# Layer 1's h split into three bf16 parts by word halves on two engines, and layer 2's edge loads issued later in a block

## The reference

```python
def _sage_conv(x, src, dst, W_l, b_l, W_r):
    agg = segment_sum(x[src], dst)
    cnt = segment_sum(ones, dst)
    return (agg / max(cnt, 1)[:, None]) @ W_l + b_l + x @ W_r

def L0(x):                       # node network
    h = relu(_sage_conv(x, src, dst, W_l1, b_l1, W_r1))      # layer 1
    h = relu(_sage_conv(h, src, dst, W_l2, b_l2, W_r2))      # layer 2
    return h @ W_out + b_out

def L1(x, edge_attr):            # edge network
    out = concat([x[src], edge_attr], axis=1)
    out = selu(out @ W1a + b1a) @ W1b + b1b
    mean = segment_sum(out, dst) / max(counts, 1)[:, None]
    h = concat([x, mean, u[0]], axis=1)
    return selu(h @ W2a + b2a) @ W2b + b2b

x = layernorm(x + L0(x))
x = layernorm(x + L1(x, edge_attr))
```

## Time and profile before

| | |
|---|---|
| median of 3 runs | 2545.67 us (2545.40 to 2546.12) |
| profiled execution | 2547.18 us |
| its span | 2545.4 us |
| mean granted TensorE clock | 0.917 of full speed |
| TensorE busy (matmuls) | 2084.5 us, 82% |
| VectorE busy | 1637.0 us, 64% |
| ScalarE busy | 1015.8 us, 40% |
| GpSimd busy | 1845.8 us, 73% |
| DMA | 342.56 MB, mean 135 GB/s |
| block of counts, load | 12 issues of 5488 KB seen, 18.7 us from issue to landing |

### The profile page before, as it was taken

How to read it: one execution, slowest core, us unless ns; L and a number is a source line. 1 busy time by engine, 2 the same in 40 slices (tenths; PEclk the granted TensorE clock), 3 DMA queues, 4 the chain that set the end, 5 groups by cost and what they waited for, 6 DMA issues and landing times. The chain is left out here.

```text
span 2545.4 us, 54296 instructions
## 1 busy us (share of the span) xinstructions
PE 2084.5 (82%) x19234; PEld 1539.5 (60%) x19234; DVE 1637.0 (64%) x3320; ACT 1015.8 (40%) x2319; POOL 1845.8 (73%) x1864
## 2 busy tenths in 40 slices
PE   1899999989989998984788888888878888867753
PEld 1555565555545555553676676777767777766753
DVE  6899999996455564554566666666666666643433
ACT  3787877874000000013344344444433444433322
POOL 5546768676777777777777777777777777777775
PEclk9999999999999999985899999998999999986665
DMA  8368786777769877824433333333333333332212
GB/s 298 111 231 224 228 264 180 250 198 134 210 208 253 237 210 232 241 59 109 123 74 74 71 80 74 77 76 72 76 77 74 80 74 74 72 71 51 51 41 46
DMA packets 524456, 342.56 MB, mean 135 GB/s; under 512 B 398996, under 2 KB 476495, under 8 KB 520781
## 3 DMA queue, kind: packets, MB, share of 16 engines
q1 hardware_dynamic: 407075, 267.01, 38.2%
q0 software_dynamic: 54240, 57.31, 10.3%
q10 hardware_dynamic: 62890, 14.87, 2.9%
HBM read 201.55 MB, written 137.36 MB: 133 GB/s over the span
## 5 line engine op out<-in xcount | busy, mean ns | idle before, releaser
L987 POOL DMA_INDIRECT A_sb<-source_terms,src_cur x1092 | 1049.1, 961 | 332.9 <-issue 327.4
L938 POOL DMA_INDIRECT sorted_edges<-pm_row,pm_to x520 | 575.4, 1107 | 183.6 <-issue 154.1
L1871 DVE TENSOR_TENSOR arena<-iota_code,arena 128x2048 f16<-128x2048 f16 (+1 forms) x392 | 435.5, 1179 | 19.6 <-PE cnt_ps L1416 17.3
L1082 ACT ACTIVATE A_sb<-cnt_ps 128x392 f32 (+1 forms) x784 | 383.8, 499 | 135.9 <-PE cnt_ps L1416 86.2
L1545 PE MATMUL agg_ps<-A_sb,arena 128*128 128x448 f16 x1911 | 378.6, 355 | 0.0
L1416 PEld LDWEIGHTS cnt_ps<-arena 128*128 128x128 f16 x3136 | 191.1, 100 | 225.7 <-issue 161.4
L1416 PE MATMUL cnt_ps<-arena 128*128 128x98 f16 x3136 | 280.3, 214 | 44.5 <-ACT A_sb L1082 27.1
L1545 PEld LDWEIGHTS agg_ps<-A_sb,arena 128*128 128x128 bf16 x1911 | 186.1, 99 | 165.0 <-issue 5.3
L1647 PE MATMUL agg_ps<-A_sb 128*65 128x48 f32 x2184 | 179.5, 243 | 123.1 <-DVE A_sb L2208 123.1
L1647 PEld LDWEIGHTS agg_ps<-A_sb 128*65 128x65 f32 x2184 | 165.7, 158 | 138.4 <-DVE A_sb L2208 130.4
L1423 PE MATMUL agg_ps<-A_sb,arena 128*65 128x448 f16 x686 | 243.3, 355 | 0.0
(11 more groups left out here) (308 smaller groups left out, 3505.7 us busy)
## 6 DMA issues: line engine op xcount, KB each, us to landing
counts_matrix<-A_sb SPq DMA_DIRECT2D x12, 5488.0 KB, 17.4
A_sb<-counts_matrix SPq DMA_DIRECT2D x12, 5488.0 KB, 18.7
arena<-in_edge_attr_dram SPq DMA_DIRECT2D x90, 256.0 KB
sorted_edges<-zrow SPq DMA_DIRECT2D x13, 1716.0 KB
arena<-sorted_edges SPq DMA_DIRECT2D x169, 128.0 KB
A_sb<-source_terms,src_cur POOLq DMA_INDIRECT x1092
overlapping_rows<-A_sb SPq DMA_DIRECT2D x1, 13056.0 KB, 39.4
pm_row<-in_edge_attr_dram ACTq DMA_DIRECT2D x46, 256.0 KB
```

The costliest lines, as they stand in the source:

```text
L938: pool.indirect_dma_start(out=sorted_d, out_offset=bass.IndirectOffsetOnAxis(ap=pm_to[:, k, j:j + 1], axis=0), in_=pm_row[:, k, j, :], in_ ...
L987: pool.indirect_dma_start(out=gath[k][:, j * F:(j + 1) * F], out_offset=None, in_=p_d, in_offset=bass.IndirectOffsetOnAxis(ap=src_cur[k][: ...
L1082: act.activation(Asb(half)[:, :, bass.ds((b * BG + k) * GROUP, GROUP)].rearrange("p b (w j) -> p b w j", j=PAIR), cnt_ps[k % 2][:, 0:SUB * ...
L1871: ins = dve.tensor_tensor(hot_rows[:, slots], iota_code[:, 0:n, :].unsqueeze(1).to_broadcast([P, AT_ONCE * SUB // 2, n, 2]), turned[:, bas ...
```

## The change

**The split.** The rounding is replaced by a cut: the first part is the upper 16 bits of each word of h, which is a bf16 number; the rest h minus this number is exact in f32, and its upper 16 bits are the second part; the rest of that gives the third. `h_rest` names the three f32 arrays (h in `hs`, the first rest in `iota_i`'s space, the second in `h1m[1]`, in the arena), and `h_top` their upper halves, read as bf16 with a stride of two. The two subtractions go to VectorE, as a new `split_h` at hot row 48 (SPLIT_AT) of superblocks 2 to 13; for block 12 behind the sort of group 17, and for block 13 behind the sum of the counts. GpSimd's `split_h` keeps three copies of upper halves into `hpart`; the second and third wait for VectorE's `rest_made`. `h_split` now counts three a block, and `store_h` waits for the third. VectorE's first subtract waits until the copies of the block before are done.

**The loads of layer 2.** ScalarE issues none ahead of the copy of `h2T` and none behind `move_agg2`. It issues one behind the copy of `h2T`, one behind the square root, and one ahead of `move_agg2`, or two there where the next superblock has four groups.

The diff, without the renaming of a semaphore and two changed totals (line numbers in the rows of the changed kernel are those after it):

```diff
--- before.py
+++ after.py
@@ -91,6 +91,7 @@
 FROM_SP = IN_STAGE1 + 3
 PLACE_AT = (16, 36)
 SLOT_AT = (32, 44)
+SPLIT_AT = 48
 END_PARTS = NSB - 3
 ENDS_IN = 16 * 2 * (END_PARTS + 2)
@@ -394,6 +395,9 @@
         st = sb("st", [CH, 4, NCH], F32)
         hr = iota_i[0:CH, :].bitcast(F32).rearrange("p (c f) -> p c f", f=H)
         zero_c = sb("zero_c", [CH, NCH], F32)
+        h_rest = [t.rearrange("p c f -> p (c f)") for t in (hs[:, :, :], hr, h1m[1])]
+        h_top = [t.bitcast(BF16).rearrange("p (n t) -> p n t", t=2)[:, :, 1] for t in h_rest]
+        h_out = [hpart[:, i].rearrange("p c f -> p (c f)") for i in range(3)]
         src_cur = [sb(f"src_cur{i}", [P, EJ], I32) for i in range(DEEP)]
         def halves(t):
@@ -586,7 +590,7 @@
                 sp.dma_start(Wedge[half * F:(half + 1) * F, half * F:(half + 1) * F], W1a[F:2 * F, :]).then_inc(w2_in, 16)
             def store_h(m, half):
-                sp.wait_ge(h_split, m + 1)
+                sp.wait_ge(h_split, 3 * m + 3)
                 sp.dma_start(by_node(h1_d, m), hs[:, :, :]).then_inc(h_stored, 16)
                 for part in range(3):
                     sp.dma_start(by_node(hp_d[part], m), hpart[:, part, :, :]).then_inc(h_stored, 16)
@@ -885,19 +889,11 @@
                 if not isinstance(m, int) or m > 0:
                     pool.wait_ge(h_stored, m * 64)
                 pool.sem_inc(pool_at, 1)
-                pool.tensor_copy(hpart[:, 0], hs[:, :, :]).then_inc(pool_dep, 1)
-                pool.wait_ge(pool_dep, m * 4 + 1)
-                pool.sem_inc(pool_at, 1)
-                pool.tensor_tensor(hr[:, :, :], hs[:, :, :], hpart[:, 0], ALU.subtract).then_inc(pool_dep, 1)
-                pool.wait_ge(pool_dep, m * 4 + 2)
-                pool.sem_inc(pool_at, 1)
-                pool.tensor_copy(hpart[:, 1], hr[:, :, :]).then_inc(pool_dep, 1)
-                pool.wait_ge(pool_dep, m * 4 + 3)
-                pool.sem_inc(pool_at, 1)
-                pool.tensor_tensor(hr[:, :, :], hr[:, :, :], hpart[:, 1], ALU.subtract).then_inc(pool_dep, 1)
-                pool.wait_ge(pool_dep, m * 4 + 4)
-                pool.sem_inc(pool_at, 1)
-                pool.tensor_copy(hpart[:, 2], hr[:, :, :]).then_inc(h_split, 1)
+                pool.tensor_copy(h_out[0], h_top[0]).then_inc(h_split, 1)
+                pool.wait_ge(rest_made, m * 2 + 1)
+                pool.tensor_copy(h_out[1], h_top[1]).then_inc(h_split, 1)
+                pool.wait_ge(rest_made, m * 2 + 2)
+                pool.tensor_copy(h_out[2], h_top[2]).then_inc(h_split, 1)
             gather_fine(0, FEW)
             pool.wait_ge(table_out, 16)
@@ -1158,14 +1154,14 @@
                 if not isinstance(m, int) or m < NSB - 1:
                     act.wait_ge(hT_turned, m + 1)
                     act.activation(hTs[:, :], t_ps[:, 0:SBN], ACT.Copy).then_inc(hT_moved, 1)
-                if s is not None and (s == 1 or LAYER2[s - 1] == 4):
-                    load_group(FIRST[s] + 2)
                 act.wait_ge(h2_turned, m + 1)
                 act.activation(h2T, t2_ps[:, 0:SBN], ACT.Copy).then_inc(h2_moved, 1)
                 if s is not None:
-                    load_group(FIRST[s] + 3)
+                    load_group(FIRST[s] + LAYER2[s] - 1)
                 act.wait_ge(var_ready, m + 1)
                 act.activation(st[:, 3, :], st[:, 2, :], ACT.Sqrt, bias=eps_t[0:CH, 0:1], scale=1.0 / F).then_inc(std_ready, 1)
+                if s is not None:
+                    load_group(FIRST[s + 1])
                 act.wait_ge(x2_turned, m + 1)
                 act.activation(x2T, cnt_ps[1][0:F, 0:SBN], ACT.Copy).then_inc(x2_moved, 1)
                 act.activation(x2all[:, bass.ds(at, 1), :, :].rearrange("p a c f -> p (a c) f"), x2c[:, :, :], ACT.Copy).then_inc(x2_kept, 1)
@@ -1173,9 +1169,10 @@
                     act.wait_ge(hT_turned, NSB)
                     act.activation(hTs[:, :], t2_ps[:, 0:SBN], ACT.Copy).then_inc(hT_moved, 1)
                 if s is not None:
-                    load_group(FIRST[s] + 4)
+                    load_group(FIRST[s + 1] + 1)
+                    if s + 1 < NSB and LAYER2[s + 1] == 4:
+                        load_group(FIRST[s + 1] + 2)
                     move_agg2(s)
-                    load_group(FIRST[s] + 5)
             def move_agg2(s):
                 act.wait_ge(agg2_ready, s + 1)
@@ -1905,6 +1902,10 @@
                     make_hot(s, half, begun, SLOT_AT[0])
                     begun = SLOT_AT[0]
                     own_terms(s - 2)
+                if s >= 2:
+                    make_hot(s, half, begun, SPLIT_AT)
+                    begun = SPLIT_AT
+                    split_h(s - 2)
                 make_hot(s, half, begun, SB_GROUPS)
             def grid(ap, f):
@@ -1928,6 +1929,14 @@
                 if m > 0:
                     dve.wait_ge(h_relu, m)
                 dve.tensor_tensor(hv[:, :, :], ht[:, :, :], grid(v_ps, H), ALU.add).then_inc(h_ready, 1)
+
+            def split_h(m):
+                dve.wait_ge(h_relu, m + 1)
+                if m > 0:
+                    dve.wait_ge(h_split, 3 * m)
+                dve.tensor_tensor(h_rest[1], h_rest[0], h_top[0], ALU.subtract).then_inc(rest_made, 1)
+                dve.wait_ge(rest_made, m * 2 + 1)
+                dve.tensor_tensor(h_rest[2], h_rest[1], h_top[1], ALU.subtract).then_inc(rest_made, 1)
             def layer(m, at=None):
@@ -2013,6 +2022,8 @@
             for q in range(IN_STAGE1, IN_STAGE1 + 3):
                 slot_group(q)
                 sort_group(q + 1)
+                if q == IN_STAGE1:
+                    split_h(NSB - 2)
             layer(NSB - 1)
@@ -2026,6 +2037,7 @@
             dve.wait_ge(layer_dve, 4 * NSB)
             inverses(0)
             dve.tensor_reduce(chk[0:CH, 0:1], all_counts, AX_X, ALU.add).then_inc(chk_made, 1)
+            split_h(NSB - 1)
             slot_group(IN_STAGE1 + 3)
             sort_group(IN_STAGE1 + 4)
             dve.wait_ge(chk_sum, 1)
```

6 lines of the change are left out of this document (3 added, 3 removed).

## The result

| | before | changed |
|---|---|---|
| median | 2545.9 us (4 runs) | 2599.9 us (4 runs, 2596.4 to 2601.6) |
| ratio | | 1.0206, 95% interval 1.0192 to 1.0221 |
| profiled execution, span | 2545.4 us | 2599.8 us |
| first scatter of group 18 | 652.02 us | 698.23 us |
| first gather | 1145.83 us | 1195.68 us |

The account below looks back on a forecast made before the run. VectorE was taken to bound the counting stage and GpSimd's scatters and gathers the rest from 652.0 us. Group 18 -1.1, loads -4.2 and hand-over -1.0 gave -6.3 us: 2545.7 to 2539.4 us, range 2531 to 2556.

Parts of the forecast that it names:

- The step that failed: Superblock 13's split: copies beside VectorE's work cost 0.4 us each, so split 11 is done at 598.8 us, 6.5 us later in the superblock.
- The step that turned it into time: Other superblocks of the counting stage: the later store and scatters cost nothing, the next `relu_h` coming some 25 us on.
- Rival C: Counting stage: each of GpSimd's three copies costs VectorE as much as a subtract, 0.9 us; 2556.2 us, slower; chance 0.16.
- The price of the copies on VectorE: Counting stage: GpSimd's three copies of a split cost VectorE 1.3 us a block, as the three casts did.
- The counting stage once the copies get in: Superblocks 2 to 12: 1.3 + 1.4 - 3.1 = -0.4 us a block, -4.4 us over 11 blocks.
- The end of split 11: In superblock 13: 6.5 us later in the superblock, 2.1 us later by the clock.
- the first scatter behind the blank: Group 16, behind the DMA that blanks `sorted_edges`: starts at 628.5 us instead of 626.41, 2.1 us later.
- Group 18: Start of its scatters, after groups 16 and 17 and a shorter split 13: 650.9 us instead of 652.02, -1.1 us.
- the sum of this part: The split's whole effect up to the start of group 18: -1.1 us.
- The hand-over's term: Before the gathers: part of GpSimd's 1.51 us wait for the stored source terms goes, -1.0 us (0 to 1.5).
- The loads' term: Layer 2: loads behind the copy of `h2T`, the block of counts having landed, end GpSimd's seven waits for slots, -4.2 us.
- 4 to 8 us at the next superblock's start, four times: Layer 2: TensorE waits this long where two loads precede `move_agg2` in superblocks 1, 4, 7 and 10, costing GpSimd nothing.

Follow-up runs that it names:

- one_input: Changed kernel plus one tiny single-input VectorE instruction behind the split's two subtracts; 2556.3 us against 2543.8 before, ratio 1.0043; on slower chips 0.9961.
- one_input_split_c: Changed kernel with a tiny single-input VectorE instruction behind the subtracts and layer 2's loads in their old places; 2549.6 us against 2541.2 before, ratio 1.0035.
- early_split_b: Changed kernel with the tiny single-input instruction, layer 2's loads in their old places and the subtracts at hot row 40; 2544.5 us against 2541.2 before, ratio 1.0017.

## Why the prediction was wrong, point by point

**The step that failed** is "six hot instructions from 584.98 us with one copy beside them ... two subtracts and the copy between them, 1.4 + 0.4, to 598.0; the last copy to 598.8 us". It prices a copy that must wait by the hot instruction in progress, as the old casts had to. In the changed kernel the copies of block 11 wait behind the second subtract, not in a run of hot instructions alone; the second copy ran from 636.89 to 642.07 us there, for 5.3 us in one other block and for 11.2 or 13.3 us in seven. In the old trace GpSimd's casts waited beside hot instructions only, and I took their 1.1 us for the rule. The page rule that the prediction put beside it (the Trainium skill, "SBUF — State Buffer", section "Who interferes with whom": the lock is held for a whole instruction) would have the copy wait 0.7 us for the subtract. The traces show 5 to 17 us; the measurement decides.

**The step that turned it into time** failed too: "In the other superblocks the later store and the later scatters cost nothing: the next `relu_h` comes some 25 us on". The prediction named what stands behind the split in SP's queue, the loads among them, and then asked only who needs `hs` next. The one who was near was VectorE, which sorts the loaded edges early in the next superblock, 13 us behind the subtracts: a split held up until then made it wait 6.6 us. Eleven such waits are the 59.1 us; in three of them the split was late because a DMA issue ahead of it had been kept out, which the prediction did not price either. Even with the cure this link has no room to spare: in `one_input` VectorE waits 4.36 us for the edges at 602.48 us, in the kernel before not at all.

**Rival C** (slower, by copies that take from VectorE) had the sign and 2556 us, but not the mechanism: the copies took no more from VectorE than forecast; GpSimd was kept out, and VectorE then waited for data. Its chance of 0.16 was spent on the price of a copy. The missing rival was the wait in the other direction.

**What held.** The price of the copies on VectorE: nine hot instructions with two copies beside them take 10.06 us in `one_input`, against 9 x 1.02 = 9.2, so 0.4 us a copy and 1.3 us for three, as taken. The subtracts: 0.68 and 0.69 us. The counting stage once the copies get in: superblock 13 begins 3.9 us earlier, 4.4 forecast. The end of split 11: 3.0 us later by the clock, 2.1 forecast, and the first scatter behind the blank at 629.8 us, forecast 628.5. Group 18: 652.2 us, forecast 650.9. Each step is right to 1.3 us, and the sum of this part is nothing instead of -1.1. These are times of the fastest of ten executions.

**The hand-over's term, -1.0 us,** came in `one_input`, where GpSimd's wait of 1.51 us for the stored source terms is gone, but partly because its last scatter ends 1.2 us later than before. In the changed kernel that wait is 2.48 us. In all, the first gather of `one_input` is at 1145.11 us, 0.7 us earlier than before where 6.3 were forecast.

**The loads' term, -4.2 us, did not come.** TensorE's 9.6 us wait for `xTs` is gone, and another stands in its place. Waits of TensorE, 716 to 1141 us, and ScalarE's queue in the changed kernel:

```profile
PE agg_ps L1512 <- ACT aggS L1179: 20.6, 5, 11.8
```

```profile
1064.17 8.07 ACTq L1151 DMA_DIRECT2D pm_ends<-in_dst_dram  x1
1072.29 0.54 ACT L1179 ACTIVATE aggS<-agg_ps 128x448 f32<-128x448 f32 x1 [15.47 <-issue]
```

The forecast had "4 to 8 us at the next superblock's start, four times"; it was 11.8 us once and 8.8 us in four. The claim behind the term, that with the loads behind the copy of `h2T` the block of counts has landed, holds for that superblock's block and not for the next one's: a load ahead of `move_agg2` waits for the scatters of group q - 5, reaches into the next superblock, and meets the next 5.5 MB, 8 us for one issue here and 11.8 us at 809.71 us in `one_input`. GpSimd's waits for slots stayed at 5.8 us in `one_input` and 7.2 us in the changed kernel, against 6.3. With the loads in their old places and the copies let in they are 2.3 us (`one_input_split_c`) and 4.0 us (`early_split_b`), and TensorE's 9.6 us wait is not in those two traces either. So it is no fixed cost of the old places, and its absence in the changed kernel need not be the moved loads' doing. From group 18 to the end of the last scatter `one_input` takes 492.2 us and `one_input_split_c` 488.3, in one trace each on two chips.

## What to carry to other kernels

Before a step is moved from GpSimd to VectorE, look at what VectorE runs right behind it: a two-input instruction of another kind ahead of a long run without gaps can keep GpSimd, its DMA issues too, out of SBUF for the whole run, and the profile books that as a long, busy GpSimd instruction. A shape that takes 0.6 us in one place and 11 us in another is such a wait, and one tiny single-input instruction at the boundary ended it here. And when a producer is made later, ask of every instruction behind its consumer in the queue, the loads above all, how soon its data are wanted.
